# A causal mask moved into idle contraction rows of an attention kernel, with its mask products cut to 64 columns and the side work of each group reordered

## What is computed

```
a = norm(x);  q, k, v = a@wq.T, a@wk.T, a@wv.T      # 16 heads of 64
q, k = rotary(q), rotary(k)
scores = where(causal, q@k.T / 8, -inf)
x = x + norm(softmax(scores) @ v -> @wo.T)
x = x + norm(ffn(norm(x)))                           # 8 experts, top 4, and a shared one
```

## Time and profile before

| | |
|---|---|
| median of 3 runs | 1211.6 us (1211.09 to 1211.76) |
| the profiled execution | 1211.64 us, its span 1209.6 us |
| PE, DVE, ACT, POOL busy, share of the span | 93%, 80%, 78%, 78% |
| attention slots 1 to 14 | about 131 to 896 us |
| second half (norms and ffn) | from about 939 us |

### The profile page before, as it was taken

How to read it: one execution, slowest core, us unless ns; L and a number is a source line. 1 busy time by engine, 2 the same in 40 slices (tenths; PEclk the granted TensorE clock), 3 DMA queues, 4 the chain that set the end, 5 groups by cost and what they waited for, 6 DMA issues and landing times. The chain is left out here.

```text
span 1209.6 us, 34888 instructions
## 1 busy us (share of the span) xinstructions
PE 1126.5 (93%) x13543; PEld 788.0 (65%) x13543; DVE 968.5 (80%) x2220; ACT 944.3 (78%) x2193; POOL 947.0 (78%) x984
## 2 busy tenths in 40 slices
PE   4689999999999999999999999999999598999996
PEld 1246777777777777777777777777777354566553
DVE  7799797887979787878879797978764559777987
ACT  3667988989797978889797979789899574766574
POOL 3478899999989999999989999999677474334463
PEclk9699999999999999999999999999999799999998
DMA  6652525253452515252543515253420200000011
GB/s 201 161 140 52 126 71 117 61 141 82 96 128 50 141 38 140 71 140 61 118 108 71 141 37 141 66 126 80 102 67 3 52 1 2 1 1 1 2 36 36
DMA packets 50660, 97.03 MB, mean 80 GB/s; under 512 B 6720, under 2 KB 23360, under 8 KB 48448
## 3 DMA queue, kind: packets, MB, share of 16 engines
q1 hardware_dynamic: 50496, 94.81, 31.6%
HBM read 58.47 MB, written 34.60 MB: 77 GB/s over the span
## 5 line engine op out<-in xcount | busy, mean ns | idle before, releaser
L827 POOL TENSOR_TENSOR Plo<-P,Phi 128x512 f16<-128x512 f32 (+3 forms) x640 | 537.5, 866 | 65.5 <-ACT P L516 62.1
L513 ACT ACTIVATE Phi<-psS 128x512 f16<-128x512 f32 (+3 forms) x768 | 393.8, 513 | 128.1 <-PE psS L368 83.3
L516 ACT ACTIVATE P<-psS 128x512 f32<-128x512 f32 (+3 forms) x640 | 316.2, 495 | 0.0
L392 PE MATMUL psO<-V,Plo 128*128 128x65 f16 x2304 | 288.6, 194 | 0.0
L388 PE MATMUL psO<-V,Phi 128*128 128x65 f16 x2304 | 287.3, 192 | 0.0
L390 PE MATMUL psO<-V,Phi 128*128 128x64 f16 x2304 | 286.4, 192 | 0.0
L365 PE MATMUL psS<-Q,K 128*128 128x512 f16 (+3 forms) x768 | 251.4, 327 | 9.6 <-DVE Plo L672 5.6
L388 PEld LDWEIGHTS psO<-V,Phi 128*128 128x128 f16 x2304 | 219.4, 98 | 56.3 <-issue 0.3
L368 PE MATMUL psS<-Q,K 65*128 65x512 f16 (+3 forms) x768 | 252.1, 328 | 0.0
L721 DVE TENSOR_REDUCE pmax<-psX 128x1 f32<-128x512 f32 x384 | 242.6, 682 | 0.8 <-PE psX L452 0.3
L390 PEld LDWEIGHTS psO<-V,Phi 128*128 128x128 f16 x2304 | 213.7, 96 | 30.9 <-issue 0.2
(11 more groups left out here) (200 smaller groups left out, 2159.0 us busy)
## 6 DMA issues: line engine op xcount, KB each, us to landing
K<-k_way SPq DMA_DIRECT2D x48, 512.0 KB, 7.0
k_way<-HL SPq DMA_DIRECT2D x64, 256.0 KB, 4.1
q_way<-HL SPq DMA_DIRECT2D x60, 256.0 KB, 3.7
Q<-q_way SPq DMA_DIRECT2D x60, 256.0 KB, 7.0
Q<-q_way SPq DMA_DIRECT2D x15, 512.0 KB, 11.8
out<-y SPq DMA_DIRECT2D x8, 256.0 KB, 2.2
y<-in_x SPq DMA_DIRECT2D x3, 512.0 KB, 11.2
hn<-in_x SPq DMA_DIRECT2D x3, 512.0 KB, 5.6
```

What stands on the lines that cost most here:

```text
L392: mm = nc.tensor.matmul(O, M.Plo[:, U % NP_, k * P:(k + 1) * P], V[:, HD:2 * HD + 1], start=False, stop=j == t, skip_group_check=True)
L513: nc.scalar.activation(M.Phi[:, U % NP_, 0:w], X, ACT.Exp, scale=SCALE)
L516: nc.scalar.activation(full, X, ACT.Exp, scale=SCALE).then_inc(S.exp_done, 1)
L827: nc.gpsimd.tensor_tensor(M.Plo[:, U % NP_, 0:w], M.P32[:, U % NP_, 0:w], M.Phi[:, U % NP_, 0:w], ALU.subtract).then_inc(S.lo_pool, 1)
```

## The change

1. K2 and Q2 now hold what the maxima need: K2 rows 0 to 63 are the high keys, Q2 rows 0 to 63 the high queries, and rows 64 to 127 are written once by ACT (`far_rows`, 16 copies in all, 8 for each buffer): row 64 is 64.0 in K2, and in Q2 zero until the maxima arrive; rows 65 to 127 of K2 have 32768 where key = row, those of Q2 have -32768 where query < row. Their product is -2^30 on the masked places of keys 65 to 127. K1 becomes (low, high) against Q1 (high, low).
2. A diagonal unit's second product is split: 128 columns with all 128 rows, the rest (if any) with 65. Its mask product shrinks from 128 to 64 columns.
3. The maxima use Q2 and K2: 65 rows off the diagonal, 128 rows on it, as products of their own, and a mask product of 65 columns.
4. `load` starts with a transfer of 128 pieces of 64 bytes that sets row 64 of Q2 to zero; the near transfers are K2 and Q2 (0.5 MB for a pair of heads), the far ones K1 twice and Q1. The sum of bytes stays.
5. The steps of the side items are new, some steps take side items first or `weighted` before `scores`, ACT and DVE have such sets too, DVE's part of V comes a step later, and the low halves on DVE are units 4, 8, 14, 16, 24, 28, 32, 45 instead of every 4th and 8th of a head.

```diff
+BIG = 32768.0
+LEFT = HD + 1
+NEAR = (48, 32)
-QK_STEPS = (1, 2, 7, 11, 16, 17, 23, 27)
-V_STEPS = (5, 24, 35, 46)
-LN_STEPS = (16, 32)
-MX_STEPS = (8, 8, 9, 10, 11, 12, 13, 14, 15, 15, 17, 18, 19, 19, 20, 20, 21, 21,
-            22, 23, 25, 25, 26, 28, 29, 29, 30, 31, 33, 34, 36, 36, 37, 38, 38, 40)
-JOIN_STEP, MT_STEP = 41, 43
-DVE_LAG = {}
-LOW_FIRST = False
-TR1_STEPS, WO_STEPS, TR0_STEPS = (10, 16), (17, 18), (33, 46)
-LO_DVE = (4, 8)
+QK_STEPS = (0, 3, 8, 10, 16, 16, 23, 27)
+V_STEPS = (5, 26, 35, 46)
+LN_STEPS = (6, 32)
+MX_STEPS = (6, 8, 9, 12, 12, 13, 14, 15, 15, 15, 16, 17, 17, 19, 20, 20, 21, 21,
+            22, 23, 24, 26, 27, 27, 29, 30, 31, 32, 32, 34, 34, 37, 38, 38, 40, 40)
+JOIN_STEP, MT_STEP = 43, 44
+DVE_LAG = {'v': 1}
+LOW_FIRST, OUT_FIRST = (1, 2, 4, 7, 9, 12, 17, 21, 22, 23, 24, 25, 29, 34, 36, 38, 44), (2, 11, 12, 27, 29, 30, 31, 34, 40, 42, 47)
+SIDE_FIRST = (0, 2, 3, 5, 6, 19, 25, 33, 35)
+WEIGHTED_FIRST = (0, 2, 6, 7, 8, 9, 10, 15, 16, 18, 19, 20, 21, 22, 24, 27, 31, 32,
+                  33, 35, 36, 39, 43, 47)
+ACT_FIRST = (1, 3, 6, 9, 15, 16, 17, 23, 27, 28, 30, 31, 35, 37, 39, 42)
+TR1_STEPS, WO_STEPS, TR0_STEPS = (10, 13), (16, 17), (44, 45)
+FAR_AT = {(-2, 2): (4, 5), (-2, 3): (6, 7), (-2, 6): (8, 9), (-2, 8): (10, 11), (-1, 20): (12, 13), (-1, 22): (14, 15)}
+LO_DVE = (4, 8, 14, 16, 24, 28, 32, 45)
...
 def lo_on_pool(u):
-    return u % NU not in LO_DVE
+    return u not in LO_DVE
...
-                mm = nc.tensor.matmul(out, M.K2[0:HD + 1, p, h, j * P:(j + 1) * P],
-                                      M.Q2[0:HD + 1, p, h, c:c + w], start=False, stop=not diagonal)
                 if diagonal:
-                    mm = nc.tensor.matmul(out[:, 0:P], M.ident16[:], M.maskT[:], start=False, stop=True)
+                    nc.tensor.matmul(out[:, 0:P], M.K2[:, p, h, keys], M.Q2[:, p, h, keys], start=False, stop=False)
+                    if w > P:
+                        nc.tensor.matmul(out[:, P:w], M.K2[0:LEFT, p, h, keys], M.Q2[0:LEFT, p, h, c + P:c + w],
+                                         start=False, stop=False)
+                    mm = nc.tensor.matmul(out[:, 0:HD], M.ident16[:], M.maskT[:], start=False, stop=True)
+                else:
+                    mm = nc.tensor.matmul(out, M.K2[0:LEFT, p, h, keys], M.Q2[0:LEFT, p, h, c:c + w],
+                                          start=False, stop=True)
...
-                        mm = nc.tensor.matmul(X[:, c:c + n * P], M.Q1[0:rows, p, h, t * P:(t + 1) * P],
-                                              M.K1[0:rows, p, h, j * P:(j + n) * P], start=True, stop=not diagonal)
-                            mm = nc.tensor.matmul(X[:, c - P:c], M.ident16[:], M.maskN[:], start=False, stop=True)
+                        if plain:
+                            mm = nc.tensor.matmul(X[:, c:c + plain * P], M.Q2[0:LEFT, p, h, own],
+                                                  M.K2[0:LEFT, p, h, j * P:(j + plain) * P], start=True, stop=True)
...
+                            nc.tensor.matmul(X[:, c:c + P], M.Q2[:, p, h, own], M.K2[:, p, h, own],
+                                             start=True, stop=False)
+                            mm = nc.tensor.matmul(X[:, c:c + LEFT], M.ident16[:], M.maskN[:], start=False, stop=True)
...
+            act.wait_ge(S.patterns, 2)
+            for n in range(2):
+                far_rows(n)
...
+                sp.dma_start(M.Q2[HD:HD + 1, p].rearrange("o h n -> o (h n)").rearrange("o (q e) -> o q e", e=HALF),
+                             M.zeros[:]).then_inc(S.near_in[0], 16)
                 for i in range(2):
                     h = slice(2 * i, 2 * i + 2)
-                    sp.dma_start(M.K1[:, p, h], krows[:, h]).then_inc(S.near_in[i], 16)
-                    sp.dma_start(M.Q1[0:HD, p, h], qrows[0:HD, h]).then_inc(S.near_in[i], 16)
-                    sp.dma_start(M.Q1[HD:P, p, h], qrows[0:HD, h]).then_inc(S.near_in[i], 16)
-                sp.dma_start(M.K2[0:HD, p], krows[0:HD]).then_inc(S.far_in, 16)
-                sp.dma_start(M.Q2[0:HD, p], qrows[HD:P]).then_inc(S.far_in, 16)
+                    sp.dma_start(M.K2[0:HD, p, h], krows[0:HD, h]).then_inc(S.near_in[i], 16)
+                    sp.dma_start(M.Q2[0:HD, p, h], qrows[0:HD, h]).then_inc(S.near_in[i], 16)
+                sp.dma_start(M.K1[0:HD, p], krows[HD:P]).then_inc(S.far_in, 16)
+                sp.dma_start(M.K1[HD:P, p], krows[0:HD]).then_inc(S.far_in, 16)
+                sp.dma_start(M.Q1[:, p], qrows[:]).then_inc(S.far_in, 16)
```

More of the change, by code:

```diff
@@ L489, in _ @@
                 U = SU * s + u
-                if s >= 0 and U <= last_unit:
+                early = s > 0 and u in SIDE_FIRST
+                first = s > 0 and u in WEIGHTED_FIRST
+                for item in at.get((s, u), []) if early else []:
+                    side(item)
+                if s >= 0 and U <= last_unit and not first:
                     scores(U)
@@ L495, in _ @@
                     weighted(U - LAG)
-                for item in at.get((s, u), []) if s <= LAST else []:
-                    side(item)
-                for item in at.get((s, u), []) if s > LAST else []:
+                if s >= 0 and U <= last_unit and first:
+                    scores(U)
+                for item in at.get((s, u), []) if not early else []:
                     side(item)
@@ L568, in x_normal, with far_rows @@
                                      bias=M.shift[:, n:n + 1]).then_inc(S.norm_later, 1)
+            def far_rows(n):
+                p, k, h = n // (2 * GH), n // GH % 2, n % GH
+                rows = (M.K2, M.Q2)[k][HD:P, p, h].rearrange("p (t i) -> p t i", i=P)
+                pattern = M.Plo[HD:P, k, 0:P].rearrange("p (o i) -> p o i", o=1)
+                nc.scalar.copy(rows, pattern.to_broadcast([HD, TT, P])).then_inc(S.far_rows, 1)
             def junk(n):
@@ L598, in _ @@
                 nc.scalar.activation(M.std[:, tiles], M.std[:, tiles], ACT.Sqrt).then_inc(S.std_ready[0], 1)
+            for n in range(2, 4):
+                far_rows(n)
             weight_hi(0)
@@ L601, in _ @@
                 U = SU * s + u
+                for item in act_at.get((s, u), []) if s > 0 and u in ACT_FIRST else []:
+                    side(item)
                 if s >= 0 and U <= last_unit:
                     exps(U)
-                for item in act_at.get((s, u), []):
+                for n in FAR_AT.get((s, u), ()):
+                    far_rows(n)
+                for item in act_at.get((s, u), []) if s <= 0 or u not in ACT_FIRST else []:
                     side(item)
@@ L806, in _ @@
                     x_reciprocal()
-                if LOW_FIRST and s >= 0 and U <= last_unit and not lo_on_pool(U % SU):
+                for Uw, n in halves_at(s, u, OUT_LAG) if u in OUT_FIRST else []:
+                    out_scale(Uw, n)
+                if u in LOW_FIRST and s >= 0 and U <= last_unit and not lo_on_pool(U % SU):
                     low(U)
@@ L814, in _ @@
                     join_max(s)
-                if not LOW_FIRST and s >= 0 and U <= last_unit and not lo_on_pool(U % SU):
+                if u not in LOW_FIRST and s >= 0 and U <= last_unit and not lo_on_pool(U % SU):
                     low(U)
-                for Uw, n in halves_at(s, u, OUT_LAG):
+                for Uw, n in halves_at(s, u, OUT_LAG) if u not in OUT_FIRST else []:
                     out_scale(Uw, n)
@@ L853, in _ @@
             nc.gpsimd.memset(M.maskT[:], 0.0)
-            nc.gpsimd.memset(M.maskN[:], 0.0).then_inc(S.consts, 1)
+            nc.gpsimd.memset(M.maskN[:], 0.0)
+            nc.gpsimd.memset(M.Plo[:, 0, 0:P], 0.0)
+            nc.gpsimd.memset(M.Plo[:, 1, 0:P], -BIG).then_inc(S.consts, 1)
             pool.wait_ge(S.consts, 1)
@@ L858, in _ @@
                                         pattern=[[-1, P]], channel_multiplier=1)
+            nc.gpsimd.affine_select(out=M.Plo[:, 0, 0:P], in_=M.Plo[:, 0, 0:P], compare_op=ALU.not_equal, fill=BIG, base=0,
+                                    pattern=[[-1, P]], channel_multiplier=1)
+            nc.gpsimd.affine_select(out=M.Plo[:, 1, 0:P], in_=M.Plo[:, 1, 0:P], compare_op=ALU.is_ge, fill=0.0, base=-1,
+                                    pattern=[[-1, P]], channel_multiplier=1).then_inc(S.patterns, 1)
             nc.gpsimd.affine_select(out=M.maskT[:], in_=M.maskT[:], compare_op=ALU.is_ge, fill=NEG, base=0,
[L861 removed]
+                                    pattern=[[1, HD]], channel_multiplier=-1)
             nc.gpsimd.affine_select(out=M.maskN[:], in_=M.maskN[:], compare_op=ALU.is_ge,
[L863 to L864 removed]
+                                    fill=NEG, base=0, pattern=[[-1, LEFT]], channel_multiplier=1).then_inc(S.consts, 1)
+            pool.wait_ge(S.patterns, 1)
+            for k, value in enumerate((MSCALE, 0.0)):
+                last = nc.gpsimd.affine_select(out=M.Plo[:, k, 0:P], in_=M.Plo[:, k, 0:P], compare_op=ALU.not_equal,
```

(7 more changed lines are left out.)

52 lines of the change are left out of this document (28 added, 24 removed).

## The result

The changed kernel is **slower** by 1%: 1221.9 us (median of 4 runs, 1219.91 to 1226.18) against 1211.3 for the kernel before beside it, a ratio of 1.0104 (95% interval 1.0082 to 1.0126). Its profiled execution took 1219.91 us, the fastest of the four, its span 1217.9. Line 365 of before is line 372 now, 388 to 392 are 401 to 405, 452 is 469 and 473, 456 is 475, 464 is 484, 709 is 749, 757 (a copy on DVE) is 797, 760 is 800 and 827 is 869.

A forecast was written before the change was run, and what follows sets the result against it. PE bounds the middle slots, with POOL close behind. 14 slots x (1.59 - 0.15) = 20.2 us, slots 15 and 0 0.4 each, start-up -0.5: 20.5 us less, to 1191.1 us; range 1185 to 1200, chance 0.55.

The forecast's parts named there:

- Part 1 and 2: PE's products: shorter masks save 1.73 us a slot, split products cost 0.14, net 1.59 less.
- (d): Mask products: weight loads pace short products, so masks keep 0.057 us and splits cost 2.7 us a slot; 1249 us, chance 0.01.
- Part 3: Who is next: POOL gets 0.74 us a slot more, 51.08 to 51.8, costing the pitch 0.15 us a slot.
- Rival (a): POOL and PE block each other, half or more of the gain lost; pitch 53.9 or more, 1201 us and up, chance 0.26.
- V parts one step later ... 0: DVE's later V parts hold a psX bank longer before the next side item; the new order covers it, cost 0.
- Part 4: Transfers and maxima: near transfers land in time for step 6, and moving the maxima's transposition from step 43 to 44 costs 0.
- I take no wait: First maxima product, 5.7 us into the slot: near transfers land by 5.0 us, so PE does not wait.
- rival (c): Each slot's first maxima item: near transfers land as late as before, 3.0 us a slot; 1231 us, chance 0.07.
- stays near 4 us; 0: Between the maxima's transposition, now step 44, and the next slot's first scores: the gap of four steps remains, cost 0.
- Part 5: The ends: slot 15 gains 0.4 us, slot 0 gains 0.4, the start-up loses 0.5, between 0 and 2.
- Two fit into its 3.18 us idle: Start-up: two of ACT's constant-row copies, like casts of 1.04 us, fit into an idle time of ACT.
- The -0.8 for slots 0 and 15: Gains at the ends: 0.4 us in slot 0, from 0 to 1.6, and 0.4 in slot 15, half of PE's 0.8.

The follow-up runs named there:

- wide_masks_old_order: The changed kernel with the step order of before and both mask products 128 columns wide again; 1219.55 us, 1.0068 of the kernel before.
- lows_old_split: Changed kernel with copy as reduction, first maxima item at step 8, second V item at 24, plus DVE's low halves as before; 1209.4 us, 0.9985.
- first_mx_at_8: The changed kernel with the first maxima item of a slot at step 8 instead of 6; 1215.09 us, 1.0033 of the kernel before.
- start_mended: Changed kernel with copy as reduction, first maxima at step 8, second V item at 24, plus start-up copies and first key transfers reordered; 1204.98 us, 0.9944.
- old_order_new_lows: New masks, tiles and transfers in the step order of before, with the new set of DVE low halves; 1249.61 us over six executions, ratio 1.0269.
- no_v_lag: The changed kernel with DVE's part of V in its own step instead of one later; 1269.32 us, 1.0482 of the kernel before.

## Why the prediction was wrong

**What bounds the kernel**: right for the kernel before, but used for more than it says. That PE was busy 53.93 of 54 us meant that every other step came just in time; it said nothing of by how much. A PE with 1.6 us less to do calls for each of them sooner.

**Part 1 and 2** were right as costs of PE's products. The mask product falls to 0.03 us, with its own weight load each, so the rival of weight loads (d) is out. The time of a weight load, for which the prediction cites the Trainium skill ("TensorE: Matmul & The Clock Gate", LDWEIGHTS), doesn't set the pace here: the loads are shown as 96 ns long and the products start 30 ns apart. The splits are cheap. Fewer rows even cost a little, which the rounding to 0.22 us hid: from start to start a product of 512 columns takes 219 ns with 65 rows and 215 with 128 (medians of 200 to 900 us), small against 1.73 us. What was mis-sized is how much of this reaches the time: in the old order 14.4 of 24 us (wide_masks_old_order), in part because the scores then wait for banks that DVE's low halves hold.

**Part 3**: POOL's sum came out near (over 463 to 571 us it was busy 102.14 of 108, 51.9 us a slot, forecast 51.8), if by luck: the forecast set its 51.08 us, of a stretch of 54, against a slot of 54.64, which makes 51.7 before any change, so its slack was smaller than stated. Rival (a) was not what happened: lows_old_split gave POOL its old sum and lost. "V parts one step later ... 0" failed, as 0.57 us a slot at the maxima product behind it. The lag is only part of that wait (4.6 of 6.1 us stay without it); it went from the maxima product when the V item was back at step 24 in place of 26, a move that the prediction doesn't mention. That the new order would hide the wait was an assumption, read from no row.

**Part 4** failed in both halves. "I take no wait": SP issues from 463.97 on, Q's transfer at 465.19, and PE begins at 470.75, 6.8 us after the first issue where 5.0 was forecast and step 6 came at 5.7. Q's 256 KB took 5.4 us to land in the median (4.1 to 6.7), where half of 7.5 was taken: the time didn't halve with the bytes. It is rival (c)'s mechanism at about an eighth of its price, 0.39 us a slot where 3.0 were stated; taken out by itself (first_mx_at_8) it gave 6.8 us. The 0 for the later join ("stays near 4 us; 0") was the costliest step, 10.1 us. It failed ahead of the transposition and not behind it: the join now stands one step before it in place of two, and holds a copy of 1.20 us. I looked at PE's items between transposition and scores, and not at DVE's four instructions ahead of them and what runs on POOL beside them. The copy costs about 1 us in nearly every slot of the changed kernel, and 5 us in a slot of other orders where POOL had its long rows of low halves there.

**Part 5**: start-up +0.5 forecast, +1.7 measured at the first exponential, inside its bounds. "Two fit into its 3.18 us idle" overlooked the table load that they bring, and "the others later" had no price, though two of those copies stand right ahead of the first exponential. The -0.8 for slots 0 and 15 didn't come: the tail was 3.0 us longer. Over the runs the time from the last slot's first exponential was 312 to 317 us, with no rule that I found.

The steps that failed are thus the three zeros, for the join, the V parts and the near transfers: they stand for 0.63, 0.57 and 0.39 us a slot, and they turned the sign. With them out and the lag gone the kernel is faster, and 1197.7 us lies within the forecast's 1185 to 1200. But the size was off as well: the pitch came to 53.71, 0.96 us less than before, where 1.44 less was forecast (1.59 - 0.15). What stays open is that last 0.5 us a slot, in short gaps that are not listed one by one, the tail, and which start-up order would give back its 1.7 us; start_mended was one try.

## What to carry to other kernels

Where one engine is full and others are near it, price a moved step by its slack, the time between its data's readiness and its first reader, for each reader, DMA issue and engine behind; a row with no wait shows that slack is over zero and not that there is any. Write tiny copies between SBUF tiles on DVE as something that doesn't contend with POOL (a reduction over one element did) before judging any order by its time: here one such copy made one order look 59 us worse and another 34. And in a slot that is nearly in balance, test halves of a change alone, since the order and the masks had opposite signs.

## What the runs showed of the hardware

I hadn't expected a copy of 128x8 to take 0.165, 1.20 or 5.3 us by what POOL does at its start; in every long case it ended some 30 ns after the end of a POOL instruction. In the changed kernel it waited so for one instruction; in the slots of 4.8 to 5.6 us (12 of 30 in old_order_new_lows and no_v_lag) for a row of five or six without a gap. The reduction of the same shape took 0.158 us beside the same POOL. The Trainium skill ("SBUF — State Buffer", Who interferes with whom) says that VectorE's copies can run in a mode that needs a port pair shared with GpSimd, taken for a whole instruction, and that a reduction on this chip never does: the trace agrees (1.20 us against 0.158). The 5.3 us show in addition that the wait can pass over several instructions of GpSimd.

The table load took 1.28 us at 5.76. The Trainium skill ("ScalarE: Activation LUTs", What ACT_TABLE_LOAD costs) gives about 1283 ns for it: the trace agrees.
